# Mixture-of-experts stage of a perceiver block: which engine splits which weight unit, and when

## The reference, cut to what matters

```python
router_logits = x @ w_router                     # 8 experts
top_w, top_i = jax.lax.top_k(router_logits, 2)
top_w = softmax(top_w)
for ei in range(8):
    hmid = silu(x @ w0[ei]) * (x @ w1[ei])       # 512 -> 1024
    out = out + gating[:, ei:ei+1] * (hmid @ wo[ei])   # 1024 -> 512
```

## Time and profile before

| | us |
|---|---|
| median of 3 runs | 684.59 |
| lowest, highest | 679.28, 684.75 |
| profiled execution | 680.1 |
| its span, first to last instruction | 678.1 |

### The profile page before, as it was taken

How to read it: one execution, slowest core, us unless ns; L and a number is a source line. 1 busy time by engine, 2 the same in 40 slices (tenths; PEclk the granted TensorE clock), 3 DMA queues, 4 the chain that set the end, 5 groups by cost and what they waited for, 6 DMA issues and landing times.

```text
span 678.1 us, 12394 instructions
## 1 busy us (share of the span) xinstructions
PE 623.4 (92%) x4593; PEld 508.5 (75%) x4594; DVE 416.2 (61%) x718; ACT 386.6 (57%) x567; POOL 245.0 (36%) x170
## 2 busy tenths in 40 slices
PE   8989999999989999899999999879966979979986
PEld 7867888888868888677888888768755758757764
DVE  7775667657767456667683447817731354764796
ACT  4589989979953344420432443427843556765760
POOL 4069987878963222340000223510220020220222
PEclk9999999999999999999999999979978979979999
DMA  8515653442423332499953310239911839939944
GB/s 316 211 63 194 203 186 133 165 154 71 139 80 88 125 109 103 156 398 388 375 181 119 125 63 0 94 131 358 368 35 21 332 103 353 360 103 338 360 154 152
DMA packets 57272, 125.54 MB, mean 185 GB/s; under 512 B 5896, under 2 KB 6664, under 8 KB 54160
## 3 DMA queue, kind: packets, MB, share of 16 engines
q1 hardware_dynamic: 51584, 115.16, 47.3%
q10 hardware_dynamic: 4368, 5.64, 2.8%
q0 software_dynamic: 1280, 4.20, 1.9%
HBM read 102.83 MB, written 22.15 MB: 184 GB/s over the span
## 4 chain that ended last, share of the span: by engine, by line
PE 69%; issue 8%; ACT 7%; DVE 6%; ACTq 4%; POOL 3%; DMA 1%; DVEq 0%; SPq 0%; POOLq 0%
PE bank L1535 14%; PE bank L1539 14%; PE bank L1538 14%; PE bank L1551 5%; PE bank L2016 3%; PE bank L1602 3%; POOL nat_lo L501 3%; PE bank L1603 2%; PE bank L1570 2%; PE bank L1571 2%; ACT e_hi L774 2%; ACTq L884 2%; PE bank L2000 1%; ACT nat_hi L618 1%; DVE hm L1441 1%
## 5 line engine op out<-in xcount | busy, mean ns | idle before, releaser
L501 POOL TENSOR_TENSOR nat_lo<-raw,nat_hi 128x512 fp32r<-128x512 f32 x104 | 136.1, 1339 | 41.8 <-ACT nat_hi L618 41.7
L549 POOL TENSOR_TENSOR e_lo<-e_raw,e_hi 128x2048 fp32r<-128x2048 f32 x8 | 36.6, 4576 | 223.4 <-ACT e_hi L774 223.4
L925 DVE TENSOR_TENSOR ct_lo<-bank,ct_hi 128x512 fp32r<-128x512 f32 x96 | 65.9, 689 | 33.2 <-ACT ct_hi L585 32.8
L618 ACT ACTIVATE nat_hi<-raw 128x512 fp32r<-128x512 f32 x104 | 64.7, 630 | 0.0
L585 ACT ACTIVATE ct_hi<-bank 128x512 fp32r<-128x512 f32 x96 | 57.0, 596 | 9.0 <-PE bank L1551 6.8
L1441 DVE TENSOR_TENSOR hm<-bank,vectors 128x512 f32<-128x512 f32 (+1 forms) x28 | 14.5, 519 | 75.9 <-PE bank L1539 35.7
L1271 DVE TENSOR_TENSOR w_lo<-w_raw,w_hi 128x2048 fp32r<-128x2048 f32 (+1 forms) x24 | 54.6, 2298 | 9.1 <-ACT w_hi L774 9.1
L1551 PE MATMUL bank<-ident,raw 128*128 128x128 f32 x384 | 57.7, 273 | 0.3
L1551 PEld LDWEIGHTS bank<-ident,raw 128*128 128x128 f32 x384 | 46.7, 140 | 12.8 <-issue 0.9
L1535 PE MATMUL bank<-turned,w_hi 128*128 128x512 f32 (+1 forms) x144 | 53.2, 370 | 1.4 <-DVE turned L1076 1.4
L1535 PE MATMUL bank<-w_hi,turned 128*128 128x512 f32 x128 | 50.7, 396 | 2.6 <-issue 2.5
(11 more groups left out here) (292 smaller groups left out, 1484.4 us busy)
## 6 DMA issues: line engine op xcount, KB each, us to landing
raw<-in_ctx_dram SPq DMA_DIRECT2D x24, 1024.0 KB, 5.0
w_raw<-in_L_ffn_w_dram SPq DMA_DIRECT2D x24, 1024.0 KB, 7.5
e_raw<-in_L_ffn_wo_dram SPq DMA_DIRECT2D x16, 1024.0 KB, 12.7
w_raw<-in_L_attn_w_dram SPq DMA_DIRECT2D x8, 1024.0 KB, 5.8
slots_x<-zeros SPq DMA_DIRECT2D x1, 8192.0 KB, 27.7
slots_y<-zeros SPq DMA_DIRECT2D x1, 8192.0 KB, 33.1
e_raw<-in_L_ffn_w_dram SPq DMA_DIRECT2D x8, 1024.0 KB, 11.6
vectors<-slots_x ACTq DMA_DIRECT2D x13, 256.0 KB, 4.6
```

The costliest lines, as they stand in the source:

```text
L501: nc.gpsimd.tensor_tensor(nat_lo[:, j, :], raw[b % 2][:, j, :], nat_hi[:, j, :].bitcast(f32), ALU.subtract).then_inc(nat_lo_ready, 1)
L618: nc.scalar.activation(nat_hi[:, j, :], raw[b % 2][:, j, :], ACT.Copy).then_inc(nat_hi_ready, 1)
L925: nc.vector.tensor_tensor(ct_lo[:, n % CR, :], src, ct_hi[:, n % CR, :].bitcast(f32), ALU.subtract).then_inc(t_lo, 1)
```

## The change

- Late units are split at the head of the full block that uses them: ACT makes the upper part of unit 5 of its own expert before the first silu and of unit 4 behind it; DVE makes the lower parts of units 2 and 3 before the first hidden half, and of unit 4 behind it. Upper parts of units 0, 1, 2 and 3 of the next expert are still made one block early, with unit 2 moved ahead of the upper part of hidden half 1.
- POOL makes two lower parts an expert, unit 5 of the block's own expert and unit 1 of the next one; DVE makes four (2, 3 and 4 of its own, 0 of the next) where it made five.
- Short blocks wait for the load of a unit and no longer for its split.
- The store of a block's output is one DMA and no longer four.
- A silu of four numbers a partition stands ahead of ACT's loops.
- Ahead of the loops the splits of units 4, 5, 2 and 3 of expert 0 are gone, and DVE makes all four lower parts of the first rows at once. In the last block DVE makes the gates (`gates_made`) behind the lower part of hidden half 0.

```diff
-        POOL_FIRST = (4, 5, 1)
+        POOL_FIRST = (1,)
...
-            with pool.Fori(1, E - 1) as e:
+            with pool.Fori(0, E - 1) as e:
                 split_e(e, POOL_UNIT)
+                split_e(e + 1, 1)
+            split_e(E - 1, POOL_UNIT)
...
-                if n in (9, 10, 11):
-                    split_e(0, (4, 5, 3)[n - 9], (xT_done, 2 * KD))
+                if n == 11:
+                    split_e(0, 3, (xT_done, 2 * KD))
...
             def expert_block(b, e, last=False):          # ScalarE
+                split_e(e, 5)
                 silu(b, 0)
+                split_e(e, 4)
                 if last:
-                    act.wait_ge(y_stored, 16 * FULL_R * b + 1)
+                    act.wait_ge(y_stored, 16 * b + 1)
                     nc.scalar.activation(drained[:, :], mhalf[:, :], ACT.Copy).then_inc(prior_stored, 1)
                 split(0)
                 silu(b, 1)
                 upper_hidden(b, 0)
                 split(1)
+                split(2)
                 upper_hidden(b, 1)
...
                 next_rows(b)
-                split(2)
                 split(3)
                 output_copied(b, D)
-                split(4)
                 act.wait_ge(y_ready, b + 2)
                 row = row_of(b) * R
-                for q in range(FULL_R):
-                    nc.scalar.dma_start(ys[bass.ds(row + q * R, R), :], yb[q * R:(q + 1) * R, :]).then_inc(y_stored, 16)
-                split(5)
+                nc.scalar.dma_start(ys[bass.ds(row, P), :], yb[:, :]).then_inc(y_stored, 16)
...
+            nc.scalar.activation(drained[:, :], mhalf[:, 0:NT], ACT.Silu)
             act.wait_ge(slots_ready, 5)
             with act.Fori(0, E - 1) as e:
...
-            for k in range(2, KD):                       # VectorE, ahead of the loops
-                first_lower_rows(k)
-            split_e(0, 2)
...
             def expert_block(b, e, last=False):          # VectorE
+                split_e(e, 2)
+                split_e(e, 3)
                 hidden(b, 0)
...
-                    gates_made()
+                split_e(e, 4)
                 split(0)
                 lower_hidden(b, 0)
+                if last:
+                    gates_made()
                 hidden(b, 1)
                 if last:
                     gathered_added(0)
...
                 lower_rows(b + 1)
-                split(1)
-                split(2)
-                split(3)
-                split(4)
-
-            split_e(0, 3)
...
-            split_e(E - 1, 5)
...
-                pe.wait_ge(e_hi_ready[j], turn_of(e, j))   # TensorE, short_up; short_down alike
+                pe.wait_ge(e_loaded[j], 16 * turn_of(e, j))
...
             pe.wait_ge(slots_ready, 4)
+            pe.wait_ge(xgT_lo_ready, KD)
             with pe.Fori(0, E - 1) as e:
```

More of the change, by code:

```diff
@@ L769, in _, with split_e @@
             act.wait_ge(b1_loaded, 16)
-            def split_e(e, j, wait):
+            def split_e(e, j, wait=None):
                 act.wait_ge(e_loaded[j], 16 * turn_of(e, j))
-                act.wait_ge(*wait)
+                if wait is not None:
+                    act.wait_ge(*wait)
                 nc.scalar.activation(e_hi[j][:, :, :], e_raw[j][:, :, :], ACT.Copy).then_inc(e_hi_ready[j], 1)
@@ L851, in short_block @@
                 row = row_of(b) * R
-                for q in range(FULL_R):
-                    nc.scalar.dma_start(ys[bass.ds(row, R), q * P:(q + 1) * P], yb[q * R:(q + 1) * R, 0:P]).then_inc(y_stored, 16)
+                nc.scalar.dma_start(ys[bass.ds(row, R), :].rearrange("t (q c) -> q t c", q=FULL_R), yb[:, 0:P]).then_inc(y_stored, 16)
             def expert_block(b, e, last=False):
@@ L1417, in _ @@
             nc.vector.tensor_copy(blocks[:, 1, :], upto_extra[:, :]).then_inc(slots_ready, 1)
-            for k in range(2):
+            for k in range(KD):
                 first_lower_rows(k)
@@ L2030, in short_down @@
             def short_down(b, e, half):
-                pe.wait_ge(e_hi_ready[4 + half], turn_of(e, 4 + half))
+                pe.wait_ge(e_loaded[4 + half], 16 * turn_of(e, 4 + half))
                 pe.wait_ge(hmT_hi_ready, 2 * b + half + 1)
@@ L2036, in short_block @@
             def short_block(b, e):
-                pe.wait_ge(xgT_lo_ready, b + KD)
+                pe.wait_ge(xgT_hi_ready, b + KD)
                 for j in range(3):
@@ L2042, in short_block @@
                 short_up(e, 3)
+                pe.wait_ge(xgT_lo_ready, b + KD)
                 rows_transposed(b + 1)
```

## The result

| | before | after |
|---|---|---|
| median, us | 683.37 | 692.77 |
| lowest, highest | 679.28, 684.75 | 692.34, 694.73 |
| profiled execution, span | 680.1, 678.1 | 694.73, 693.0 |

Ratio 1.0153, 95% interval 1.0103 to 1.0204: slower by 1.5%, where I forecast no change at 682.9 and gave up to 692.0. (A fourth run of the kernel before brought its median from 684.59 to 683.37.) The two traces are single executions, that of before near the low end of its runs and that of after the highest of its own, so they differ by 14.9 us where the medians differ by 9.4.

What follows compares the result with a forecast made beforehand. Blocks were taken as bound by PE except at a few waits. Gains of 20.7 us against losses of 19.0 gave -1.7 on the profiled 680.1, or 682.9 on the median; own range 676 to 688, wider range 671 to 692.

Steps and rivals of the forecast that it cites:

- The mechanism: Full blocks: DVE's split waits on the port shared with POOL and ends about 2.14 us behind POOL's split.
- Clock, the term that failed: Full blocks, behind the new idle times of PE: no clock loss counted in the sum, 0 us.
- rival (B): Three full blocks: new idle times bring the clock down, 3 us a block, 9 in all, giving 693.9 us; chance 0.19.
- The new stalls: Before the first down product: 1.9 us each in four full-behind-short blocks (7.6), 2.2 each in three full-behind-full (6.6).
- R: ACT's step after the store behind a full block, two register reads and a branch: 1.7 us, bounds 0.40 and 1.93.
- Gains: Short blocks' stalls, first block and clock together: 20.7 us less.
- the two stall terms: PE's idle before the hidden half of short blocks: 8.9 us less behind full (three), 5.4 less behind short (two).
- the first block: No DVE split beside the scatters, so the next rows' load comes 2.4 us earlier and PE follows.
- The clock of the short blocks: Short blocks get granted clock back behind shorter idle times: 4 us gained, between 0 and 5.8.
- rival (C): The silu ahead doesn't remove table loads; five places lose 1.28 us again, 6.4, giving 689.3 us; chance 0.08.
- The last block: DVE's row operations and unit 4 wait for POOL's unit 5, gathers start later: 4.8 us lost.
- Rival (A): Order between DVE and POOL falls better or blocking is shorter: 666.7 us, half of it 674.8; chance 0.21.

Runs made afterwards that it cites:

- the version with unit 5 late: Kernel after, but unit 4 split a block early again, DVE's splits reordered, and POOL making only unit 5: 662.38 us, ratio 0.9659 to before.
- the run with unit 4 first: Kernel after, with ACT making unit 4 before the first silu and unit 5 behind it, and DVE making unit 0 last: 670.05 us, ratio 0.9771.
- single stores: Kernel before with only one store DMA a block and the silu ahead of ACT's loops: 668.39 us, ratio 0.982.
- row read early: The version with unit 5 late, with ACT also reading the store's row number ahead of the output copy: 655.46 us, again 655.23 (ratios 0.9634, 0.9618).

## Why the prediction was wrong, point by point

**The mechanism was right.** One wait went, another came, at the place and by the lock that I had named: DVE's split blocked by POOL's, ending 2.14 to 2.16 us behind it, in all seven blocks. The runs without POOL's work and with the order turned round show that it is this lock, and that who comes first has it. The Trainium skill's rule (SBUF — State Buffer, "SBUF: two separate sides") agrees in both directions. I had applied it to operations with two inputs in SBUF alone; in the last block four `TENSOR_SCALAR` with one such tensor and a column of numbers were held up as well (3.99 us beside POOL, where the same four take 0.90 in the version with unit 5 late). The same section names DVE's two-port modes beside two inputs in SBUF as takers of the lock; that these four run in such a mode no row shows.

**Clock, the term that failed.** I put the clock behind the new idle times at zero, and in rival (B) let it fall only from some 3.8 us on. That bound came from two kinds of place, 4.6 (fell) and 2.9 (didn't), and I read a rule into them. The same trace spoke against it: there are two waits of 2.9 us, and behind the other one the clock fell (window of the kernel before, from that wait to the block's end):

```profile
509.96:515.80 5.84, 5.42 (x102) 4.25 (x106) 0.98 (x2) 1.32 (x4) 0.00 (x0) 0.71 0.12 22
```

I had even counted 1.3 us for this block among the gains. In the kernel after it fell behind 2.6 to 2.7 us in three of four blocks, and without POOL's split behind 1.9 to 2.0 in three of three (0.79 each). The filled idle time prices it: 1.5 to 1.6 us a block in six blocks, some 9.4; in the table, where it is what is left when the idle times are taken off, it is +8.4. Rival (B) was this mechanism, and that its 9 is near this total is luck: I gave it three blocks at 3 us, it took six at half of that. Half of my miss is here.

**The new stalls, 4.6 us short.** The single store of a short block costs 1.06 to 1.20 us of issue, not 1.80 / 4 = 0.45: dividing a row of four by four took the cost as one of count. That of a full block took 0.37 to 0.45, as reckoned. So behind short blocks POOL started 4.61 to 4.75 us behind the block's start, not 3.89. Behind full blocks it was 6.00 to 6.20 against 5.64, as R, with up to 2.09 us, lay above my upper bound of 1.93. That bound came from a place where I took the reads to be hidden under a split.

**Gains.** -18.2 against -20.7, every one at its place: the two stall terms fell short by the same store and R, the first block (-2.3) came as said, with the last two scatters at 0.97 and 0.96 us. The clock of the short blocks gave -3.7 for my 4, in part by luck: I took idle times of 1.7 us to be harmless, but behind 1.94 and 1.93 it still fell (0.70 in two of three short blocks). The table loads went, rival (C) fell. But I costed that part for the short blocks only; without the silu ahead the change would have made 20 loads, not 13, and 24 us more. I had looked at the loads that are there, not at what the moved copy would bring.

**The last block, 3.1 us short.** Two of them are the other side of the -2.0 for leaving the loop: PE idled 0.48 there and not 2.50, so it began the last block 1.02 us ahead of ACT's store (658.39 and 659.41), where before it began 0.99 behind it (651.41 and 650.42). ACT was not late: from the end of the store's issue to its split it took 1.65 us, for which I had 1.9. So POOL's unit 5 started 5.0 us behind the block's start, not 3.3. The rest stands behind POOL: DVE had four `TENSOR_SCALAR` more behind the lock, which end 0.68 after it, and from unit 4's split to the first gather another 0.85 us pass (672.10 to 672.95). The gathers started 14.6 us behind the block's start (672.95 - 658.39), not 11.3. PE too waited: 2.79, 0.62, 1.12, then 2.50 for the last lower part.

**Rival (A)** is what the order of engines would have given, and the run with unit 4 first gives it: 0.977, near the gain I worked out for it (666.7 / 684.6 = 0.974). That the totals meet so well is luck in part, as that run also moves DVE's unit 0 and pays 4.1 us at three blocks' heads and, against the version with unit 5 late, 7.5 in the last block.

What stays open: why PE idles up to 4 us on leaving the loop over the experts in kernels whose seventh full block has no stall (3.9 to 4.1 with unit 5 late, 3.6 with unit 4 first; 0.48 in after, 2.0 with the stall filled). And which of two equal idle times brings the clock down: behind 2.78 and 2.77 us at the same place it was 1.00 and 0.80. No run here was made for it.

## What to carry to other kernels

Moving an elementwise split with both inputs in SBUF from DVE to GpSimd took nothing off DVE's path here where both were needed at the same time: lay out which of them comes to the shared port first, and put operations of DVE that read PSUM beside GpSimd's. Price a new idle time of PE with the clock behind it: here 2.7 us of idle cost 4.3 in three of four places. Look for places that speak against a rule before you use it: one was in the trace of before. And when an operation is moved in front of another on ACT, ask which table loads the new order makes, not only which ones the old one had.

## What the runs showed of the hardware that I had not expected

- The granted clock fell behind idle times of PE of only 1.9 to 2.0 us (0.79 in three full blocks without POOL's split, 0.70 in two of the three short blocks of after behind a full one), but not behind 1.3 to 1.5 in nine places (before, single stores, row read early). Between 1.9 and 2.9 us it went either way: 1.00 in the third of these short blocks (1.97), behind 2.78 in after and behind 2.90 in before, 0.80 and 0.71 behind 2.77 and 2.92.
- A filler of ten matmuls in the idle time held the clock at 1.00 in all windows read behind it, with 2.0 us of idle still left behind full blocks. In a short block of the same run, with no filler, it fell behind 1.94 us (0.68).
- One `dma_start` of a short block's rows, regrouped from four partition groups into 32 rows, takes 1.06 to 1.20 us to issue; one of 256 KB that is plain takes 0.36 to 0.45.
- The first copy of a loop body gets a table load too (1.28 us), if the table at the loop's entry is that of another function.
